# Operands and weights split earlier around the down blocks and at the end of the first FFN of a fused adaLN-attention-FFN layer

## The reference

```python
c = x @ W.T + 2 * routed_low_rank(x)                # 8 experts, top 2
a = hidden_approximation(c)                         # 6 orders, width 128
x = x + a + (silu(c @ gate_w.T) * (c @ up_w.T)) @ down_w.T      # first FFN, 1248 hidden
c2 = x @ W2.T + b + 2 * ((x @ A[slot]) @ B[slot])   # low rank by token group
h1, h3 = lora_linear(c2, w1, A1, B1), lora_linear(c2, w3, A3, B3)
x = x + lora_linear(silu(h1) * h3, w2, A2, B2)      # second FFN, 1376 hidden
```

## Time and profile before

| what | us |
|---|---|
| median of 3 runs | 456.35 (456.27 to 457.39) |
| the profiled execution, whole | 457.57 |
| its span, first to last instruction | 455.9 |
| TensorE busy (98% of the span) | 446.5 |
| VectorE busy (71%) | 324.5 |
| ScalarE busy (46%) | 211.6 |
| mean granted TensorE clock, share of full | 0.996 |

### The profile page before, as it was taken

One profiled execution on the slowest core, in us unless ns is written; L12 is line 12 of the kernel. 1 busy time (PEld: TensorE's weight loads), 2 busy tenths in 40 slices (PEclk: granted clock), 3 DMA queues, 4 the chain that ended last, 5 costly groups with the idle time before them and its releaser, 6 DMA issues.

```text
span 455.9 us, 5562 instructions
## 1 busy us (share of the span) xinstructions
PE 446.5 (98%) x2009; PEld 364.0 (80%) x2009; DVE 324.5 (71%) x471; ACT 211.6 (46%) x324; POOL 29.2 (6%) x51
## 2 busy tenths in 40 slices
PE   8999999999999999999997999999999999999997
PEld 7788888888777888768884888888888888888886
DVE  5755799657987678886568555989963468887731
ACT  6364442355664456553644555556542124565300
POOL 1004100000010100004300000000000000000000
PEclk9999999999999999999999899999999999999999
DMA  8407700136574564637243101222110232112022
GB/s 288 136 0 224 187 1 0 34 94 156 123 197 121 138 155 127 169 89 192 70 128 107 39 0 47 63 58 76 42 47 24 69 92 65 46 47 69 1 93 92
DMA packets 20299, 42.28 MB, mean 93 GB/s; under 512 B 2672, under 2 KB 2944, under 8 KB 20272
## 3 DMA queue, kind: packets, MB, share of 16 engines
q1 hardware_dynamic: 16992, 34.35, 23.4%
q0 software_dynamic: 3280, 7.58, 9.5%
HBM read 39.82 MB, written 2.10 MB: 92 GB/s over the span
## 4 chain that ended last, share of the span: by engine, by line
PE 87%; DVE 8%; ACT 2%; DMA 1%; issue 1%; ACTq 0%; DVEq 0%
PE PS L1676 14%; PE PS L1541 14%; PE PS L1542 14%; PE PS L1543 14%; PE PS L1677 13%; PE PS L1678 13%; DVE G L922 2%; DVE WU L922 1%; DMA raw<-in_pieces 1%; ACT G L481 1%; PE PS L1862 1%; PE PS L1604 1%; DVE X L1377 1%; ACT WU L481 1%; DVE T L1107 1%
## 5 line engine op out<-in xcount | busy, mean ns | idle before, releaser
L1676 PE MATMUL PS<-HT,WU 128*128 128x512 f32 x266 | 103.8, 390 | 0.7 <-DVE WU L922 0.7
L1677 PE MATMUL PS<-HT,WU 128*128 128x512 f32 x266 | 103.6, 390 | 0.0
L1678 PE MATMUL PS<-HT,WU 128*128 128x512 f32 x266 | 103.5, 389 | 0.0
L481 ACT ACTIVATE WU<-raw 128x256 fp32r<-128x256 f32 (+2 forms) x55 | 49.0, 897 | 34.0 <-PE PS L1678 18.1
L922 DVE TENSOR_TENSOR WU<-raw,WU 128x256 fp32r<-128x256 f32 (+2 forms) x56 | 56.5, 1013 | 5.1 <-ACT WU L481 5.0
L1676 PEld LDWEIGHTS PS<-HT,WU 128*128 128x128 f32 x266 | 50.0, 188 | 11.7 <-DVE WU L922 1.5
L481 ACT ACTIVATE PS<-PS 128x512 f32<-128x512 f32 x46 | 26.8, 582 | 68.6 <-PE PS L1678 65.2
L1678 PEld LDWEIGHTS PS<-HT,WU 128*128 128x128 f32 x266 | 49.9, 188 | 10.5
L1677 PEld LDWEIGHTS PS<-HT,WU 128*128 128x128 f32 x266 | 50.0, 188 | 10.1
L922 DVE TENSOR_TENSOR G<-T,G 128x1024 fp32r<-128x1024 f32 (+2 forms) x46 | 43.9, 968 | 18.0 <-ACT G L481 17.1
L481 ACT ACTIVATE G<-T 128x1024 fp32r<-128x1024 f32 (+2 forms) x47 | 39.8, 856 | 20.0 <-DVE T L1038 6.8
(11 more groups left out here) (170 smaller groups left out, 705.9 us busy)
## 6 DMA issues: line engine op xcount, KB each, us to landing
raw<-in_pieces SPq DMA_DIRECT2D x87, 256.0 KB, 3.7
raw<-in_parts SPq DMA_DIRECT2D x14, 512.0 KB, 3.6
raw<-in_parts POOLq DMA_DIRECT2D x14, 384.0 KB, 4.9
X<-in_x SPq DMA_DIRECT2D x8, 256.0 KB, 5.1
out_x<-X SPq DMA_DIRECT2D x7, 256.0 KB, 2.0
su_raw<-in_stk_up POOLq DMA_DIRECT2D x6, 192.0 KB, 2.7
T<-in_lora_b POOLq DMA_DIRECT2D x16, 32.0 KB, 2.1
ga_raw<-in_lora_a POOLq DMA_DIRECT2D x8, 32.0 KB, 3.4
```

Source lines behind the costliest of these rows:

```text
L481: return nc.scalar.activation(o, i, ACT.Copy)
L1676: pe.matmul(bank, w[:, 1, cols], hi, start=start and kc == 0, stop=False, skip_group_check=not start)
L1677: pe.matmul(bank, w[:, 0, cols], low, start=False, stop=False, skip_group_check=not start)
L1678: mm = pe.matmul(bank, w[:, 0, cols], hi, start=False, stop=kc == 1, skip_group_check=not start)
```

## The change

It has four parts. (1) In `steady1` VectorE splits the second part of the next block's weights before T4, and the additions to X of a down block come after it. (2) In the block ahead of the first down block (q + 1 is `first_down`), the first weight part of the second down block is split too; loads are ordered so (`BLOCK_PIECES`), first pieces of blocks are loaded only in the columns used, and each sum region is loaded ahead of its second piece instead of its first. TensorE runs p1 of both down blocks first in `enter_down`. (3) In `enter_down` the operands T2, B21, T3, B22 and T4 are summed, copied and split one at a time instead of in pairs, with semaphore counts from the tables `G_SUM` and `G_SPLIT`; the second weight part of the second down block is split in two halves, the first of which, through `early`, lets p6 start. (4) S13 and S2 are loaded ahead of the tail weights and split in block 12, where the second weight part of block 13 comes first too; tail weights and W2 follow in block 13 and under the tail. Two more raw slots (4 and 5) in the sum region of even blocks hold them. `x1` interleaves additions and splits, and ScalarE's wait for all four down banks of a half goes.

```diff
@@ -85,15 +85,19 @@
 
 
 SLOT = [p % RING for p in range(P_FFN)]
-P_BLOCK = []
+
+P_ONE, P_TWO, BLOCK_PIECES = {}, {}, []
 for _q in range(len(BLOCKS)):
-    P_BLOCK.append(len(SLOT))
-    SLOT += [0, 1] if _q % 2 == 0 else [3, 2]
-P_TAIL = len(SLOT)
-P_S13 = P_TAIL + 2
+    for _step in ([], [(0, _q), (0, _q + 1), (1, _q)], [(1, _q)], [(0, _q), (1, _q)])[
+            3 if BLOCKS[_q][0] == "u" else 1 + BLOCKS[_q][1] % 2]:
+        (P_ONE, P_TWO)[_step[0]][_step[1]] = len(SLOT)
+        BLOCK_PIECES.append(_step)
+        SLOT.append(((0, 1), (3, 2))[_step[1] % 2][_step[0]])
+P_S13 = len(SLOT)
 P_S2 = P_S13 + 1
-P_W2 = P_S2 + 4
-SLOT += [0, 1, 2, 3, 0, 1, 2, 3, 0, 1, 2]
+P_TAIL = P_S2 + 4
+P_W2 = P_TAIL + 2
+SLOT += [0, 1, 4, 5, 3, 2, 0, 1, 4, 5, 3]
 P_CHUNK, P_HALF, P_FULL = [], 0, 0
...
 B11, B21, B22, T1, T2, T3, T4 = range(7)
 B12 = T4
+
+
+
+
+G_SUM, G_SPLIT = {}, {}
+for _c in range(TAIL):
+    _sums = (["T1"],) if _c % 2 == 0 else (["T2", "T3"], ["T4"]) if _c % 4 == 1 else (["T2"], ["T3"], ["T4"])
+    _splits = ((["T1"],) if _c % 2 == 0 else (["T2", "T3"], ["B21", "B22"], ["T4"]) if _c % 4 == 1
+               else (["T2"], ["B21"], ["T3"], ["B22"], ["T4"]))
+    for _table, _groups in ((G_SUM, _sums), (G_SPLIT, _splits)):
+        for _names in _groups:
+            _n = max(_table.values(), default=0) + 1
+            for _name in _names:
+                _table[_c, _name] = _n
+for _c in range(TAIL, C1):
+    for _h in range(2):
+        G_SPLIT[_c, _h] = max(G_SPLIT.values()) + 1
...
             return 16 * SLOT[:p + 1].count(SLOT[p])
 
         def before_in_slot(p):
-            return max(q for q in range(p) if SLOT[q] == SLOT[p])
+
+            return max([q for q in range(p) if SLOT[q] == SLOT[p]] or [P_TWO[LAST - 1]])
 
         def term_count(h, m):
             return 2 * (m - 1) + h + 1
...
@@ -429,13 +449,17 @@
                 else:
                     sp.dma_start(raw_slot(P_CW + c), pieces[P_CW + c]).then_inc(raw_in[SLOT[P_CW + c]], 16)
             for p in range(RING, PIECES):
-                if p in P_BLOCK:
-                    q = P_BLOCK.index(p)
+                k, q = BLOCK_PIECES[p - P_FFN] if P_FFN <= p < P_S13 else (None, None)
+                if k == 1:
                     if q > 1:
-                        sp.wait_ge(w_ready, P_BLOCK[q - 2] + 2)
+                        sp.wait_ge(w_ready, P_TWO[q - 2] + 1)
                     sp.dma_start(sum_region(q), parts[q][:, 0:1024]).then_inc(sum_in[q % 2], 16)
                 sp.wait_ge(w_ready, before_in_slot(p) + 1)
-                sp.dma_start(raw_slot(p), pieces[p]).then_inc(raw_in[SLOT[p]], 16)
+                if k == 0:
+                    a11 = slice(256 * (q % 2), 256 * (q % 2) + 256)
+                    sp.dma_start(raw_slot(p)[:, a11], pieces[p][:, a11]).then_inc(raw_in[SLOT[p]], 16)
+                else:
+                    sp.dma_start(raw_slot(p), pieces[p]).then_inc(raw_in[SLOT[p]], 16)
             for n, (h, c, cols, _) in enumerate(OUTPUTS):
 
                 sp.wait_ge(out_ready, n + 1)
...
@@ -651,28 +672,70 @@
 
             def steady1(q):
 
+                c = number(q - 1) if is_up(q - 1) else None
+                odd = c is not None and c % 2 == 1
                 part1_hi1(q + 1, p4_done, q)
                 copy_bc1(q, *c_free(q - 1))
-                g_first(q)
+                if odd:
+                    two_hi(c, ("T2", "T3"), (T2, 1), T[:, 6:8, :])
+                elif c is not None:
+                    two_hi(c, ("T1",), (B11, T1), T[:, 2:7:4, :])
                 copy_e1(q)
-                g_later(q, 2)
+                if odd:
+                    b2_hi(c)
+                if first_down(q + 1):
+                    part1_hi1(q + 2, p1_done, q + 1)
                 part2_hi1(q + 1)
                 silu1(q, 0)
-                g_later(q, 3)
+                if odd:
+                    t_one_hi(c, "T4", T4, T[:, 2, :])
                 next_a(q)
                 silu1(q, 1)
 
             def enter_down(q):
 
+                c = number(q - 1)
                 copy_ab1(q, *b_free(q - 2))
+                t_one_hi(c, "T2", T2, T[:, 6, :])
+                b_one_hi(c, 0, B21)
+                copy_e1(q)
+                t_one_hi(c, "T3", T3, T[:, 7, :])
+                copy_bc1(q, *c_free(q - 1))
+                b_one_hi(c, 1, B22)
+                copy_ab1(q + 1, *b_free(q - 1))
+                t_one_hi(c, "T4", T4, T[:, 2, :])
+                act.wait_ge(p4_done, q)
+                part2_hi1(q + 1)
+
+            def last_but_one(q):
                 part1_hi1(q + 1, p4_done, q)
-                g_first(q)
+                part2_hi1(q + 1)
+                copy_bc1(q, *c_free(q - 1))
                 copy_e1(q)
-                g_later(q, 2)
+                s13_hi()
+                s2_hi(0)
+                silu1(q, 0)
+                s2_hi(1)
+                s2_hi(2)
                 copy_ab1(q + 1, *b_free(q - 1))
+                silu1(q, 1)
+                s2_hi(3)
+
+            def last(q):
                 copy_bc1(q, *c_free(q - 1))
-                part2_hi1(q + 1)
-                g_later(q, 3)
+                for h in range(HALVES):
+                    tail_g_hi(TAIL, h)
+                copy_e1(q)
+                tail_hi(0)
+                tail_hi(1)
+                silu1(q, 0)
+                for k in range(2):
+                    w_hi(P_W2 + k, W2[k])
+                silu1(q, 1)
+                for h in range(HALVES):
+                    tail_g_hi(C1 - 1, h)
+                for k in range(2, KC):
+                    w_hi(P_W2 + k, W2[k])
 
 
...
@@ -1089,8 +1135,13 @@
                 V.tensor_tensor(two, two, three, ALU.add).then_inc(sums_in, 1)
 
             def part2_lo1(q):
-                dve.wait_ge(hi_w, P_BLOCK[q] + 2)
+                dve.wait_ge(hi_w, P_TWO[q] + 1)
                 k, w = q % 2, WU[:, q % 2]
+                if not is_up(q) and not first_down(q):
+
+                    lo(w[:, 1, 768:1536], raw_flat[:, 2816:3584], w[:, 0, 768:1536]).then_inc(early, 1)
+                    lo(w[:, 1, 0:768], raw_flat[:, 2048:2816], w[:, 0, 0:768]).then_inc(w_ready, 1)
+                    return
                 lo(w[:, 1, PART2[k]], raw_flat[:, RAW2[k]], w[:, 0, PART2[k]]).then_inc(w_ready, 1)
 
             def tail_lo(j):
...
-            def block1(q):
-                up = is_up(q - 1)
-                c = number(q - 1) if up else None
-                pair = up and c < TAIL and c % 2
-                if first_down(q):
-                    g_sum(c)
+            def steady1(q):
+                c = number(q - 1) if is_up(q - 1) else None
+                odd = c is not None and c % 2 == 1
+                if c is None:
+                    x_out(q - 1, "c")
+                else:
                     mul0_1(c)
-                    sums1(q + 1)
-                    part1_lo1(q + 1)
-                    g_lo1(c, 1)
-                    g_lo1(c, 2)
-                    g_sum4(c)
-                    add_b1(q)
-                    g_lo1(c, 3)
-                else:
-                    if not up:
-                        x_out(q - 1, "c")
+                    if odd:
+                        t2_sum(c)
+                        t3_sum(c)
                     else:
-                        mul0_1(c)
-                        if c < TAIL:
-                            g_sum(c)
-                    sums1(q + 1)
-                    part1_lo1(q + 1)
-                    if up and c >= TAIL:
-                        g_lo1(c, 0)
-                        g_lo1(c, 1)
-                    elif up:
-                        g_lo1(c, c % 2)
-                    add_b1(q)
-                    if pair:
-                        g_lo1(c, 2)
-                        g_sum4(c)
-                if not is_up(q):
-                    x_out(q, "a")
+                        t1_sum(c)
+                sums1(q + 1)
+                part1_lo1(q + 1)
+                if odd:
+                    two_lo(c, "T2", (T2, 1), T[:, 6:8, :])
+                elif c is not None:
+                    two_lo(c, "T1", (B11, T1), T[:, 2:7:4, :])
+                add_b1(q)
+                if odd:
+                    two_lo(c, "B21", (B21, 1), T[:, 2:4, :])
+                    t4_sum(c)
+                if first_down(q + 1):
+                    part1_lo1(q + 2)
                 add_d1(q)
-                if pair and not first_down(q):
-                    g_lo1(c, 3)
                 part2_lo1(q + 1)
+                if odd:
+                    one_lo(c, "T4", T4, T[:, 2, :])
                 if is_up(q):
                     mul1_1(number(q))
                 else:
+                    x_out(q, "a")
                     x_out(q, "d")
                     x_out(q, "b")
+
+            def enter_down(q):
+                c = number(q - 1)
+                t2_sum(c).then_inc(g_summed, 1)
+                mul0_1(c)
+                one_lo(c, "T2", T2, T[:, 6, :])
+                t3_sum(c)
```

(121 more changed lines are left out.)

159 lines of the change are left out of this document (56 added, 103 removed).

## The result

The changed kernel takes 449.75 us (median, 449.47 to 450.24), the kernel before 456.31 in the same comparison (455.31 to 457.39): ratio 0.986, 95% interval 0.983 to 0.988. That is 6.6 us faster, where 9.2 were forecast; the predicted 447.2 is 2.6 too low and inside the range. The profiled execution took 449.48, its span is 447.8 us, 8.1 less than before and 1.1 above the 446.7 predicted.

A forecast was written before the change was run, and what follows sets the result against it. TensorE, 98% busy, bounds the kernel, with 11.16 us recoverable. Gains 1.7 + 1.75 + 5.8 - 0.1, say 9.2 us, take the span from 455.9 to 446.7, the median to 447.2; forecast 445.9 to 448.6, range 445.0 to 450.6.

The forecast's parts named there:

- (a): steady1, block 2: weight split ahead of the T4 split ends at 122.16, 0.35 us early, so the wait is gone.
- (b): Blocks 3 to 5: early weight split removes the wait at 134.66, but a later sum load costs 0.15 us.
- The term of 0.15: Product waiting for add_b1(3): about 0.04 us late plus 0.11 refill, taking the median landing of GpSimd's load, 125.2.
- none worth 0.3 at p3(3): Sign to look for: no wait as large as 0.3 us in front of product p3(3).
- (c): enter_down: single operands leave p3(4) 0.65 us late plus 0.11 refill, 0.76 us; other operands in time.
- the chain t + 3.37 against t + 2.72: enter_down, p2(4) due at t: copies, B22 split, sums1(5), add_b1(4) end at t + 3.37; p3(4) due at t + 2.72.
- (d): part2_lo1(5) in halves: half ends by 141.7, p6(5) due at 142.5, no wait; whole would be just due.
- (e): End of first FFN: moved splits remove base_0's wait and clock fall; all 5.90 us won, less 0.1.
- from the span to the median: Last step: span 446.7, plus 1.67 around it gives 448.4; profiled execution 1.2 above the median, so median 447.2 us.
- everything recovered: Rival, blocks 3 to 5 and 9 to 11: p3 waits filled by undercounted margins; 445.2 us; chance 0.12.
- Late sums: Rival: accumulating load lands later than its median; at 5.9 both groups lose 1 us more, 449.2; at 6.9, 451.2; chance 0.17.
- Hand-over still waits: Rival: block 13, tail or a W2 load late, 1 to 2 us, clock falls again; 448.2 to 451 us; chance 0.13.

The follow-up runs named there:

- e3: Changed kernel with the sum loads of blocks 4 and 10 first, sums1 of enter_down earlier, and block 13's add_d1 ahead of the second tail weight split; 447.05 us.
- b1: Kernel before, with only part2_lo1 of the next block put ahead of the T4 split; 454.50 us.
- e2: Changed kernel, with sums1(q + 1) of enter_down moved from behind the B22 split to behind the B21 split; 448.02 us.
- e4: Changed kernel, with TensorE's order in enter_down put back to p1(4), p5(4), p1(5); 449.57 us.
- e5: Changed kernel, with enter_down's operands T2 and T3, and B21 and B22, summed, copied and split in pairs again; 449.23 us.
- e7: Changed kernel, with pieces and the second down block's p1 in the old order, block 5's first weight part copied and split inside enter_down; 449.93 us.
- e8: e3 with the operands of enter_down in pairs and sums1 ahead of both pair splits; 448.02 us.
- e6: e3 with the second weight part of blocks 5 and 11 split whole, p6 waiting for all of it; 447.23 us.
- o1: Changed kernel with the first FFN's old end: old load order, four slots, S13, S2 and W2 split late; x1 interleaving stays; 454.56 us.
- b2: Kernel before, with only the first addition of x1(1) moved ahead of the last stack piece and the W2 splits; 455.01 us.
- b4: Kernel before, with two needless 512-wide VectorE additions between the W2 splits and x1(1); 458.68 us.

## Why the prediction was right, and where its sizes were off

**What bounds the kernel.** Right. Counting starts against a pace of 0.2267 found 11.16 us, and e3, with nearly all holes filled, has a span 10.7 below before. The prediction read the list of waits too short, though: beside its two releasers (3.8 us) the list of before has

```profile
PE PS L1676 <- DVE T L1107: 0.8, 2, 0.4
PE PS L1541 <- DVE G L922: 0.8, 1, 0.8
```

and one of 0.2. That makes 5.6, half of the loss.

**(a) Weights before T4.** Right: block 3 starts on time, and b1 shows the two waits gone with this edit alone.

**(b) The early piece.** The mechanism was right to the step: the sum load behind block 5's piece, GpSimd's load 5 us later, sums1(4) waiting, p3(3) late. The term of 0.15 measured 0.49 (0.38 and refill) and 0.50; its sign "none worth 0.3 at p3(3)" did not come true. Start to start, SP to GpSimd took 4.06 us, not 3.88, sums1 began 5.02 after that load, not 4.9, and the whole first FFN was 0.17 later, so sums1 began at 125.67, not 125.2; and add_b1's hand-over to TensorE, 0.06 us (128.44 to 128.50), was left out. With no slack left behind sums1 every 0.1 counted. Over the executions this landing spreads: p3(3) or p3(9) was 0.05 to 0.95 late in e2, e4 and e5. As a gain the part is nothing (e7), which the prediction did not say: it charged the cost to the sum but never set it against the 0.42 that the early piece saves in the changed kernel (e7).

**(c) Operands one by one.** The 0.76 at p3(4) was forecast from the chain t + 3.37 against t + 2.72, and measured 0.65 + 0.11. What it did not see is that one of the steps, sums1, could stand in a hole, and that pairs would do as well with it in place (e5). The Trainium skill's two rules (VectorE: DVE Perf Modes, The TRN2 errata, for larger pieces; Perfetto Trace Analysis, Optimizing Scalar/DVE Operations, for breaking up to release others sooner) are both seen here: the first in the lengths (one copy and split of 1024 take 2.29 us, two of 512 take 2.62), the second in e8. The order around the operands decides: pairs 0.5 ahead in e5, 1.0 behind in e8, by medians. In each trace TensorE waits for one late chain (add_b1 in the changed kernel, the pair's split in e5), while VectorE still has a hole of 0.82 and 1.03 us ahead of it.

**(d) The halves.** Right: just due without them (e6, 0.10 and 0.07 late).

**(e) The end.** Right in the sum: 5.85 measured for 5.80, and o1 shows the wait come back with the old end. One short delay was larger: p4(13) cost 0.22 for 0.1. The walk gave 238.0 for the end of x1(0); it ended at 238.85, still before its use.

**The sum.** The step that was off is the last, from the span to the median. The loss behind the wait of base_0 at half clock was taken out of a median that held it only in part. It was 1.6 in the profiled execution, where the prediction's rivals had 1.9: the twelve starts from 250.04 to 254.49 take 4.45 us, and pace and one refill would be 2.83. In the experiments the kernel before shows a mean granted clock of 0.996 in 21 of 49 executions and 1.00 (one 0.999) in 28; in the largest set the medians of the two kinds are 457.35 and 455.92. The profiled one had been of the first kind, 1.2 above its median, which the text noticed and did not question. So of the 2.55 between 447.2 and 449.75, 1.1 are terms of the span (0.68 late sums, 0.17 the later start, 0.12 at p4(13), the rest under 0.1 each), 1.2 is this step, and 0.27 the place of the profiled execution among those of the changed kernel. The result is inside the range of 445.0 to 450.6, but above the narrower forecast of 445.9 to 448.6. Of the rivals *everything recovered* did not come. *Late sums* has a number near the result, 449.2, but by its mechanism only 0.68 of its 2 us came; most of the rest is the step above. *Hand-over still waits* did not come beyond the 0.22 at p4(13), and the granted clock stayed at 1.00.

## What to carry to other kernels

On an engine that is 98% busy, count starts against the pace between two known points: this gave the whole loss here, and the gain of each edit to a tenth. When a load is put ahead on a queue in order, look at what its wait holds back, not at the load; ask next whether an operation in a chain that is late could stand in a hole before it. Before a loss seen in one execution is taken off the median, see in the granted clocks of the others whether all of them have it.

## What the runs showed of the hardware

Behind a wait of TensorE at the end of the first FFN its clock fell from 2.4 to 1.2 GHz in some executions of a kernel and not in others. By the mean granted clock of each execution it fell in none of 12 where the longest of these waits was 1.36 us (b2), in 1 of 9 with 1.83 (b1), in 21 of 49 with 2.19 (before), in 8 of 12 with 2.19 (o1), and in 8 of 9 with 3.04 (b4). So it came more often with longer waits: none of 12 and 8 of 9 stand clear of 21 of 49 (0.005 and 0.03 by an exact test), 1 of 9 and 8 of 12 do not. Each length is that of one profiled execution, where it fell is seen in the traces of before and b4 alone, and why it falls in one execution and not in the next of the same kernel stays open.

At half clock a 512-column matmul starts every 0.42 to 0.43 us instead of 0.227. A wait of TensorE also costs a refill that no list of waits shows: 0.10 to 0.11 us behind most of those in blocks 2 to 13, 0.07 to 0.08 at p6(4) in e5 and e8.
